# Sixteen heads of eight in two attention layers: ScalarE takes the differences of every fourth turn

## The reference

```python
q = (x @ Wq).reshape(B, N, 16, 8).transpose(0, 2, 1, 3)
k = (context @ Wk).reshape(B, M, 16, 8).transpose(0, 2, 1, 3)
v = (context @ Wv).reshape(B, M, 16, 8).transpose(0, 2, 1, 3)
scores = jnp.einsum('bhid,bhjd->bhij', q, k) * scale
scores = jnp.where(context_mask[:, None, None, :], scores, max_neg)
attn = jax.nn.softmax(scores, axis=-1)
out = jnp.einsum('bhij,bhjd->bhid', attn, v)
return out.transpose(0, 2, 1, 3).reshape(B, N, DIM) @ Wo
```

## Time and profile before

| what | value |
|---|---|
| time, median of 3 runs | 1211.19 us (1211.14 to 1211.82) |
| time of the profiled execution | 1207.48 us |
| span of the profiled execution | 1205.7 us |
| TensorE busy | 1095.7 us, 91% of the span |
| VectorE busy | 690.1 us, 57% |
| ScalarE busy | 531.1 us, 44% |
| GpSimd busy | 463.7 us, 38% |
| the turns of `l2_xattn` | from about 821 to 878 us of the span |
| the turns of `l3_attn` | from about 1010 to 1075 us of the span |

### The profile page before, as it was taken

The page is one execution under the profiler, slowest core; times in us unless marked ns, Lnnn a source line. Parts: engine busy times, 40 slices in busy tenths (PEclk is TensorE's granted clock), DMA queues, the critical chain, the costliest instruction groups (busy, mean ns, idle before and its releaser), DMA issues. The chain is left out here.

```text
span 1205.7 us, 22755 instructions
## 1 busy us (share of the span) xinstructions
PE 1095.7 (91%) x8723; PEld 771.8 (64%) x8740; DVE 690.1 (57%) x2079; ACT 531.1 (44%) x1377; POOL 463.7 (38%) x551
## 2 busy tenths in 40 slices
PE   6999989899986788898999899989999999998996
PEld 5877858567762255576577566755657775566685
DVE  5554552355449936886688467728842126775522
ACT  6434333276646653355445453404443332454432
POOL 7969730033335643684487250012000004032423
PEclk9999999899996689999999999989999999999998
DMA  5000060432119201000000030001021100010312
GB/s 165 1 5 2 1 227 1 140 99 61 37 59 278 75 2 45 1 1 1 1 1 1 1 74 1 2 1 36 2 78 36 36 18 17 1 40 1 123 51 76
DMA packets 55083, 54.17 MB, mean 45 GB/s; under 512 B 19472, under 2 KB 45840, under 8 KB 53952
## 3 DMA queue, kind: packets, MB, share of 16 engines
q1 hardware_dynamic: 54048, 50.84, 13.8%
q0 software_dynamic: 928, 1.88, 0.5%
HBM read 44.08 MB, written 8.63 MB: 44 GB/s over the span
## 5 line engine op out<-in xcount | busy, mean ns | idle before, releaser
L482 POOL TENSOR_TENSOR ln_rstd<-ln_ve,ln_half 128x4 f32<-128x4 f32 x26 | 26.5, 1018 | 253.3 <-DVE ln_ve L457 253.2
L678 ACT ACTIVATE scratch<-bank 128x512 f32<-128x512 f32 x96 | 52.3, 595 | 76.7 <-PE bank L566 76.7
L630 DVE TENSOR_REDUCE scratch<-bank 128x4 f32<-128x512 f32 x96 | 61.6, 683 | 13.5 <-PE bank L2870 7.7
L1267 ACT ACTIVATE scratch<-bank 128x512 f32<-128x512 f32 x64 | 37.8, 596 | 65.2 <-PE bank L1223 65.1
L1286 DVE SCALAR_TENSOR_TENSOR x_res<-bank,scratch,x_res 128x128 f32<-128x128 f32 x64 | 18.0, 345 | 80.7 <-PE bank L1233 80.7
L1233 PEld LDWEIGHTS bank<-weights,scratch 128*128 128x128 f32 x512 | 59.5, 192 | 7.2 <-issue 6.9
L3130 POOL TENSOR_TENSOR scratch<-scratch 128x16 f32<-128x16 f32 x16 | 50.6, 3164 | 33.4 <-DVE scratch L3526 24.9
L2148 POOL TENSOR_TENSOR scratch<-scratch 128x512 f32<-128x512 f32 x32 | 33.2, 1039 | 75.7 <-DVE scratch L2349 75.7
L636 DVE TENSOR_TENSOR scratch<-bank,scratch 128x512 f32<-128x512 f32 x96 | 61.4, 681 | 0.0
L1233 PE MATMUL bank<-weights,scratch 128*128 128x128 f32 x512 | 59.6, 275 | 0.0
L1223 PE MATMUL bank<-xnT,weights 128*128 128x512 f32 x128 | 57.8, 594 | 0.7 <-ACT xnT L1256 0.7
(11 more groups left out here) (627 smaller groups left out, 2927.1 us busy)
## 6 DMA issues: line engine op xcount, KB each, us to landing
scratch<-conv_kernels SPq DMA_DIRECT2D x8, 1024.0 KB, 11.0
weights<-e_l_ffn_w SPq DMA_DIRECT2D x20, 256.0 KB, 2.9
scratch<-e_l_ffn_w SPq DMA_DIRECT2D x4, 1024.0 KB, 14.3
values<-scratch SPq DMA_DIRECT2D x8, 512.0 KB, 2.6
scratch<-values SPq DMA_DIRECT2D x8, 512.0 KB, 4.3
weights<-w_l_ffn SPq DMA_DIRECT2D x1, 3698.0 KB, 12.4
scratch<-e_l_ffn_w SPq DMA_DIRECT2D x4, 768.0 KB, 6.9
weights<-w_l_attn SPq DMA_DIRECT2D x1, 2560.5 KB, 8.6
```

What stands on the lines that cost most here:

```text
L630: self.nc.vector.tensor_reduce(self.top[:, n % 4, :], self.by_head(self.core.ps[n % 4][:, :]), AX_X, ALU.max, negate=True).then_inc(self.t ...
L678: self.nc.scalar.activation(self.prob_of(n), self.by_head(self.core.ps[4 + n % 2][:, :]), ACT.Exp, scale=scale) \
L1267: nc.scalar.activation(hT[u % 2][:, i, :], ps[UP_BANKS[i]][:, :], act_func) \
```

## The change

The turns with `n % 4 == 3` have their differences taken by ScalarE. VectorE still finds the largest scores of all turns. For such a turn ScalarE runs four instructions of 128 by 128 instead of VectorE's one of 128 by 512, since the amount added is one number per partition and head, and an activation takes one such bias at a time. They stand in ScalarE's queue behind the exponentials of the even pair before and ahead of `act_outT` and `act_outs`. A semaphore of its own, `shift_act`, counts them, and TensorE waits for that one or for the old one (`wait_shifted`). The order of pairs and the banks are the same. Both layers are changed.

```diff
-    def __init__(self, core, c, wo, more=None, o=None):
-        self.core, self.nc, self.wo = core, core.nc, wo
+    def __init__(self, core, c, wo, more=None, o=None, shifted_act=None):
+        self.core, self.nc, self.wo, self.shifted_act = core, core.nc, wo, shifted_act
...
+    def by_act(self, n):
+
+        return self.shifted_act is not None and n % 4 == 3
+
+    def wait_shifted(self, pe, n):
+
+        if self.by_act(n):
+            pe.wait_ge(self.shifted_act.sem, self.shifted_act.at(n // 4))
+        else:
+            pe.wait_ge(self.shifted.sem, self.shifted.at(n if self.shifted_act is None else 3 * (n // 4) + min(n % 4, 2)))
+
     def pe_free(self, pe, p):
         for n in (2 * p, 2 * p + 1):
             if n >= 4:
-                pe.wait_ge(self.shifted.sem, self.shifted.at(n - 4))
+                self.wait_shifted(pe, n - 4)
...
     def pe_turn(self, pe, p):
         for n in (2 * p, 2 * p + 1):
-            pe.wait_ge(self.shifted.sem, self.shifted.at(n))
+            self.wait_shifted(pe, n)
...
     def dve_shift(self, dve, p):
         for n in (2 * p, 2 * p + 1):
+            if self.by_act(n):
+                continue
...
+    def act_shift(self, act, n):
+        act.wait_ge(self.tops.sem, self.tops.at(n))
+        for i in range(4):
+            a = self.nc.scalar.activation(self.shift[:, n % 4, i * P:(i + 1) * P], self.core.ps[n % 4][:, i * P:(i + 1) * P],
+                                          ACT.Identity, bias=self.top[:, n % 4, i:i + 1])
+        a.then_inc(self.shifted_act.sem, self.shifted_act.up())
+
...
         for p in range(self.STEPS + 3):
             if p < self.STEPS:
                 self.act_exp(act, p, scale)
+                for n in (2 * p + 2, 2 * p + 3):
+                    if n < 2 * self.STEPS and self.by_act(n):
+                        self.act_shift(act, n)
             if p % 2 == 0 and 0 <= (p - 4) // 2 < B:
                 self.act_outT(act, (p - 4) // 2, 7)
...
-    sm = SmallHeads(core, c, wo)
+    sm = SmallHeads(core, c, wo, shifted_act=core.count("shift_act"))
...
-    sm = SmallHeads(core, c, wc)
+    sm = SmallHeads(core, c, wc, shifted_act=core.count("shift_act"))
```

## The result

Each kernel was timed eleven times. Two of the changed kernel's runs, 1314.74 and 1431.78 us at a mean granted clock of 0.827 and 0.738, were in a slow state and are left out; the median of its other nine is 1215.76 us, against 1210.56 for the kernel before. The ratio of the means is 1.0038 with a 95% interval of 1.0021 to 1.0055: slower by 4.6 us (2.5 to 6.7). Single runs scatter by several us, more than the cost sought, so I measure a layer in the trace.

The account below looks back on a forecast made before the run. The prediction took TensorE to set the pace, with VectorE second. Terms of 0.70, 0.90 and 1.03 us made 2.63 us slower, added to the median of 1211.19 for 1213.8 us; range of 8 in 10, 1211.5 to 1216.3.

Parts of the forecast that it names:

- delay D of `act_outT`: In ScalarE's queue, four activations of 0.257 us each put off the copy that TensorE's projection needs: 1.03 us.
- `l2_xattn`, steady, 5 batches: In steps 4 to 12 of `l2_xattn`, TensorE waits 0.14 us a batch for the late copy: 0.70 us.
- `l2_xattn`, end: In step 14 of `l2_xattn`, nothing covers the late copy; the whole delay less 0.13 us: 0.90 us.
- `l3_attn`, steady: In steady batches of `l3_attn`, the delay stays under the 1.20 us of cover and costs nothing.
- `l3_attn`, end: In step 14 of `l3_attn`, nothing covers the late copy, so the whole delay counts: 1.03 us.
- two margins: How much later the copy may come in steady batches without cost: 0.89 us in `l2_xattn`, 1.20 us in `l3_attn`.
- The 0.13 us: At the end of `l2_xattn`, VectorE's last differences are late for TensorE's last turn; 0.13 us to regain, once.
- The cheap: ScalarE's four activations delay the copy by only 0.64 us; cost 1.15 us, 1212.3 us in all; chance 0.22.
- the dear ScalarE: ScalarE's four activations, or a wait for late largest scores, delay the copy by 1.44 us; cost 6.7 us, 1217.9; chance 0.13.
- VectorE as the bound: Odd pairs in both layers come 0.60 us sooner each; the kernel is 6.5 us faster, 1204.7 us; chance 0.06.
- The largest scores: ScalarE's new wait for VectorE's largest scores stays hidden, with 0.33 us of cover in `l2_xattn`, 0.09 us in step 14.
- the third rival, the clock: At the end of a layer, TensorE's clock falls, costing 1.7 us on top of the forecast, 1215.5 us; chance 0.09.

Follow-up runs that it names:

- `l2_only`: The changed kernel with the change in `l2_xattn` alone, `l3_attn` left as before: `l2_xattn` 64.66 us, `l3_attn` 78.38 us.
- `both`: Against the changed kernel, VectorE keeps all differences and ScalarE's four activations read a constant, output unused: `l2_xattn` 65.41 us, `l3_attn` 82.84 us.
- `double`: The changed kernel with ScalarE's four activations run twice, the second time to a spare tile: ratio 1.0163, `l2_xattn` 71.90 us, `l3_attn` 86.54 us.
- `after_again`: The changed kernel once more, nothing altered: ratio 1.0023 to the kernel before, `l2_xattn` 64.70 us, `l3_attn` 79.40 us.

## Why the prediction was right, and what it missed

**The total.** The forecast was 1213.8 us, 2.6 over the kernel before, with 1211.5 to 1216.3 as its wide range. The measured 1215.76 us lies near the top of that and above the narrow range of the forecast itself, 1213.3 to 1214.5. It stays in the wide range because that had room for one fall of the clock. The difference that was measured, 4.6 us (2.5 to 6.7) and then 2.8 us (0.9 to 4.8), takes in the 2.63 both times, the first time barely. The sum is borne out by the stretches of the two layers, and not by this total.

**The terms.** All were right to 0.1 us.

| term | forecast | measured |
|---|---|---|
| delay D of `act_outT` | 1.03 us | 1.00, and 0.03 in the copy itself |
| `l2_xattn`, steady, 5 batches | 0.14 us each, 0.70 | 0.15 each, 0.75 |
| `l2_xattn`, end | 0.90 us | 1.63 - 0.75 = 0.88 |
| `l3_attn`, steady | 0 | 0 |
| `l3_attn`, end | 1.03 us | 1.06 |
| sum in the two layers | 2.63 us | 2.69 |

The sum was made of a duration and two margins, and the experiments moved D to 0.50, 1.17 and some 2 us and found the margins in the same place. That VectorE's relief is worth nothing in the steady part is shown by taking it alone. The 0.13 us that the prediction set down as regained by the relief has a second cause: with the copy late, the last turn comes behind VectorE's last differences whether VectorE is relieved or not, as the run without relief shows.

**The rivals.** The cheap and the dear ScalarE fell with the 1.00 us. VectorE as the bound fell with the relief alone, which was worth 0.13 us where that rival gives 0.60 us a batch. The largest scores were never late to ScalarE: no wait stands ahead of the new activations.

**What was mis-sized** is the third rival, the clock, to which I gave a chance of 0.09, as if it and the forecast were one or the other, though its own text says "on top of the forecast". It does come on top, in some executions. Of fourteen profiles, seven have the full delay at the end of `l2_xattn` (the changed kernel four times, `l2_only`, `both`, `double`), and five of these have `l2_ffn` longer by 1.7 us (four) or 3.4 us (one). The seven others have 118.56 or 118.57 us without exception. Five of seven against none of seven comes up by chance once in a hundred such draws (21 of 2002). But ten of these profiles had suggested the idea; of the four taken to test it, both with the delay have the fall and both without have not, which comes up by chance once in six. For the changed kernel alone it is three of four, some 1.3 us on average beside the 2.7, which makes about 4 us, between the two measured, 4.6 and 2.8 us.

I had held against it that TensorE was busy for only 3.07 of 4 us from 874 to 878 without a fall. That row shows one thin stretch behind a fuller one, 3.65 us from 870 to 874; the change made that one thin too. That two thin stretches matter where one does not is a reading, and no run shows it: in two of the seven profiles with the delay both are thin and the clock holds.

**What stays open.** That the delay brings the fall is an association over fourteen profiles, not a cause shown. In the third and fourth profile of the changed kernel the clock falls about 1.4 us behind the head of `l2_ffn`. In `after_again`, `both` and `double` it falls only some 8 us behind the head, and I can't say why a wait so far ahead should matter there. No kernel was tried that fills the wait with work for TensorE; the program runs such filler matmuls (L134, `keep_clock_bf`) in these two layers only behind step 16, in both kernels alike. The longer fall at the head of `l3_attn` in `both` is a single case. With 2.69 us in the layers and 1.3 for the falls, 0.6 us of the 4.6 in the first set has no place; its interval covers that.

## What to carry to other kernels

In this case work moved to an engine with time to spare cost what it put off there. Look up which result behind it in that queue is wanted soonest, and by how much: here 0.89 and 1.20 us of margin against 1.03 us of work decided one layer each way, while the 44% that ScalarE was busy said nothing. The same four instructions one place later cost a quarter as much. Look at the last steps by themselves, where the work that covered a wait has run out: some seven tenths of the cost (0.88 + 1.06 of 2.69 us) lay in one step of each layer. And where single runs scatter by more than the effect, marks in the trace measure a layer to 0.05 us, unless the clock falls in it otherwise than usual, as in `both`.

## What the runs showed of the hardware

The stretch of a layer repeats to 0.04 us in three profiles of the kernel before (`l2_xattn` 63.02 to 63.04, `l3_attn` 78.35 to 78.38), two of them from different chips, while what stands ahead of these layers scatters by 6 us. What stands behind them, from the head of `l3_xattn` to the end of the span, took 130.4 to 131.5 us in the first profiles and on chip 3, and 140.0 to 141.0 us on chips 11 and 13, with either kernel.

A fall of the clock in `l2_ffn` cost in steps of 1.7 us: 118.57, 120.25 and 121.94 us for the same layer. At the head of `l3_attn` the clock falls in every one of the fourteen profiles, with either kernel: from 4 to 6 us behind the head the granted clock is 0.50 to 0.55, though TensorE's longest idle time in the 8 us ahead of that (kernel before) is 0.70 us. The 78.35 us of that layer has one such fall in it.

A 128x128 copy takes 0.27 us behind exponentials, 0.28 or 0.29 right behind two activations that read PSUM with a bias operand, 0.30 behind four and 0.34 behind eight, and 0.26 behind four that read SBUF. Four of the first kind put it off by 1.00 us, four of the last by 1.17.
